# Soft mixture-of-experts stage: moving the softmax-maximum turns and the denominator products to other places of the TensorE order

## The reference, cut to what matters

```
x = layernorm(x) * norm_g + norm_b
se = (layernorm(slot_embeds) * slot_g + slot_b) * scale          # 16 experts x 64 slots
logits   = einsum('bnd,esd->bnes', x, se)
dispatch = softmax(logits, axis=1)                               # over the tokens
combine  = softmax(logits over all 1024 slots)                   # over experts and slots
slots = einsum('bnd,bnes->besd', x, dispatch)
gate  = gelu(slots @ Wg + bg);  up = slots @ Wu + bu             # 256 hidden features
eout  = (gate * up) @ Wd + bd
out   = einsum('bns,bso->bno', combine, eout);  x = x + tanh(g) * out
```

## Time and profile before

| | |
|---|---|
| timed runs | 1477.87, 1479.05, 1482.19 us; median 1479.05 |
| profiled execution, span of core 0 | 1498.2 us (no other time of that execution is at hand) |
| PE busy | 1377.6 us, 92% of the span |
| PEld busy | 1171.5 us, 78% |
| DVE busy | 953.4 us, 64% |
| ACT busy | 1012.3 us, 68% |
| POOL busy | 523.2 us, 35% |
| mean granted TensorE clock | 0.982 |

### The profile page before, as it was taken

How to read it: one execution, slowest core, us unless ns; L and a number is a source line. 1 busy time by engine, 2 the same in 40 slices (tenths; PEclk the granted TensorE clock), 3 DMA queues, 4 the chain that set the end, 5 groups by cost and what they waited for, 6 DMA issues and landing times. The chain is left out here.

```text
span 1498.2 us, 33716 instructions
## 1 busy us (share of the span) xinstructions
PE 1377.6 (92%) x12029; PEld 1171.5 (78%) x12029; DVE 953.4 (64%) x2374; ACT 1012.3 (68%) x2019; POOL 523.2 (35%) x510
## 2 busy tenths in 40 slices
PE   5898699899999999999999999988999999876985
PEld 4887588788888888888888888877778888755773
DVE  6998767666766767667667666552455555654455
ACT  5887487577677676776776767647788888633552
POOL 3112355322322322323223223302235555635553
PEclk9999899999999999999999999999999999998998
DMA  8300100399940000000000000022000000022236
GB/s 221 88 1 1 58 2 1 77 176 102 102 30 2 2 1 2 2 2 2 2 2 1 2 1 2 1 73 57 1 29 14 17 16 16 30 69 63 76 97 174
DMA packets 124980, 60.46 MB, mean 40 GB/s; under 512 B 41945, under 2 KB 120241, under 8 KB 124690
## 3 DMA queue, kind: packets, MB, share of 16 engines
q1 hardware_dynamic: 120274, 48.92, 18.2%
q0 software_dynamic: 4544, 9.38, 1.9%
HBM read 28.84 MB, written 29.44 MB: 39 GB/s over the span
## 5 line engine op out<-in xcount | busy, mean ns | idle before, releaser
L1349 DVE SCALAR_TENSOR_TENSOR hidden<-psU,b_cols,gelu 128x512 f32<-128x512 f32 x256 | 191.4, 750 | 170.1 <-ACT gelu L1474 104.9
L1474 ACT ACTIVATE gelu<-psG,b_cols 128x512 f32<-128x512 f32 x256 | 176.2, 689 | 109.6 <-PE psG L142 96.2
L1296 POOL TENSOR_TENSOR combine_sum<-combine_sum,combineT 128x512 f32<-128x512 f32 x48 | 63.3, 1319 | 294.9 <-ACT combineT L1488 294.9
L1325 POOL TENSOR_TENSOR dispatchT<-dispatchT,dispatch_inv 128x512 f32<-128x512 f32 x64 | 67.7, 1057 | 232.6 <-DVE dispatch_inv L1453 232.6
L1608 PE MATMUL psU<-w_down,hidden 128*64 128x128 f32 x2048 | 123.4, 273 | 0.0
L1608 PE MATMUL psDown<-w_down,hidden 128*64 128x128 f32 x2048 | 122.7, 273 | 0.0
L1861 POOL TENSOR_TENSOR probs<-probs,row_sum 128x512 f32<-128x512 f32 x64 | 66.2, 1035 | 143.6 <-DVE row_sum L1974 142.6
L1608 PEld LDWEIGHTS psU<-w_down,hidden 128*64 128x64 f32 x2048 | 113.2, 137 | 1.3 <-issue 1.2
L1608 PEld LDWEIGHTS psDown<-w_down,hidden 128*64 128x64 f32 x2048 | 113.9, 137 | 0.1
L140 PE MATMUL psG<-slots_hi,w_gate_hi 128*128 128x512 f32 x256 | 105.9, 414 | 1.1 <-ACT gelu L1474 0.6
L2038 ACT ACTIVATE probs<-psS,neg_max 128x128 f32<-128x128 f32 x256 | 91.2, 384 | 22.8 <-DVE neg_max L1971 18.4
(11 more groups left out here) (406 smaller groups left out, 3617.6 us busy)
## 6 DMA issues: line engine op xcount, KB each, us to landing
sorted_x<-empty_rows SPq DMA_DIRECT2D x1, 12736.0 KB, 77.5
tile_rows<-sorted_x SPq DMA_DIRECT2D x78, 65.0 KB
sorted_x<-empty_rows SPq DMA_DIRECT2D x1, 4544.0 KB, 29.9
expert_ys<-expert_y SPq DMA_DIRECT2D x16, 256.0 KB, 3.7
x<-in_x SPq DMA_DIRECT2D x8, 256.0 KB, 5.9
ctx<-in_ctx SPq DMA_DIRECT2D x8, 256.0 KB, 5.9
w_gate_raw<-in_L_ffn_Wg SPq DMA_DIRECT2D x1, 2048.0 KB, 10.9
w_up_raw<-in_L_ffn_Wu SPq DMA_DIRECT2D x1, 2048.0 KB, 16.1
```

Of the source, the lines that this page charges most:

```text
L1325: pool.tensor_tensor(e[:], e[:], over(rb[:], SEQ, 2), ALU.mult).then_inc(s["eb_normed"], 1)
L1349: dve.scalar_tensor_tensor(hid[e][:, half, :], U[half][:], bcol[:, 1, 4 * ch + 2 * e + half:][:, 0:1], gel[half][:], ALU.add, ALU.mult).th ...
L1474: act.activation(gel[half][:], G[half][:], ACT.Gelu, bias=bcol[:, 0, 4 * ch + 2 * e + half:][:, 0:1]).then_inc(s["gelu"], 1)
```

## The change

It moves work; no product, copy or reduction is added or removed. There are three moves.

- Scores: `AHEAD` goes from `(), (), (0,), (1, 2), (3,), (4, 5), (6,), (7,)` to `(), (), (0, 1), (2, 3), (4, 5), (6,), (7,), ()`, so that chunk 7 makes no score chunk, and the maximum over all eight is there when chunk 7 begins.
- Maxima: in chunk 7, `top` is turned right behind the turn of dispatch, into `M[:, 0]`; DVE's `mtok` stands between `expert_out` of the chunk before and the first `hidden`; the spread stands between `gate_up` of the second expert's halves, into `M[:, 1]`, and ACT's copy to `mb` between the last two gelu.
- Denominators: their products stand behind the last `gate_up` and ahead of the slots product, and go into `DN`; DVE's two instructions follow directly behind its last `hidden`; the first `down` of the chunk waits for the reciprocal.

In the head of octet -1, which has no experts' work, order and banks stay as they were.

```diff
-    AHEAD = ((), (), (0,), (1, 2), (3,), (4, 5), (6,), (7,))
+    AHEAD = ((), (), (0, 1), (2, 3), (4, 5), (6,), (7,), ())
...
+        def top_bank(o):
+            return M[:, 0, :] if has_core(o) else G[0][:]
+        def max_bank(o):
+            return M[:, 1, :] if has_core(o) else G[1][:]
...
 (vector engine, a chunk in order)
                     if has_core(o) and exists(o, ch, -1):
                         expert_out(k - 1, 1, (ch - 1) % CH)
+                    if ch == CH - 1 and has_head(o) and has_core(o):
+                        top_max(o)
...
                         hidden(k, 1, ch, 0)
                         hidden(k, 1, ch, 1)
+                    if has_core(o) and ch == CH - 1:
+                        need(dve, s["den"], o + 1)
+                        need(dve, s["x_new"], o)
+                        dve.reciprocal(ra[:], DN[:, 0, 0:OP]).then_inc(s["den_inv"], 1)
+                        need(dve, s["den_inv"], o + 1)
+                        dve.tensor_scalar(ra[:], ra[:], c.gates[:, 1:2], None, ALU.mult).then_inc(s["den_gated"], 1)
...
-                    if ch == CH - 1 and has_head(o):
-                        need(dve, s["top_t"], o + 2)
-                        need(dve, s["mb"], o + 1)
-                        dve.tensor_reduce(mtok[:], G0, AX.X, ALU.max).then_inc(s["mtok"], 1)
+                    if ch == CH - 1 and not has_core(o):
+                        top_max(o)
...
-                    if has_core(o) and ch == CH - 1:
-                        need(dve, s["den"], o + 1)
-                        need(dve, s["x_new"], o)
-                        dve.reciprocal(ra[:], U[0][:, 0:OP]).then_inc(s["den_inv"], 1)
...
 (scalar engine)
+            def max_rows(o):
+                need(act, s["mb"], o + 2)
+                need(act, s["ct_sub"], 8 * (o + 1))
+                act.copy(mb[:], max_bank(o)).then_inc(s["mb_ready"], 1)
...
+                        if ch == CH - 1 and has_head(o):
+                            max_rows(o)
                         gelu(k, 1, ch, 1)
...
 (tensor engine)
+            def top_turned(o):
+                need(pe, s["lb_max"], 8 * (o + 2))
+                for t in range(OP):
+                    last = pe.transpose(top_bank(o)[:, t * P:(t + 1) * P], top[:, t * P:(t + 1) * P], c.ident[:])
+                last.then_inc(s["top_t"], 1)
+            def top_spread(o):
+                need(pe, s["mtok"], o + 2)
+                for t in range(OP):
+                    last = pe.matmul(max_bank(o)[:, t * P:(t + 1) * P], mtok[:, t:t + 1].to_broadcast([P, P]), ident_r[:],
+                                     start=True, stop=True)
+                last.then_inc(s["mb"], 1)
+            def denominators(o, k):
+                need(pe, s["ct_summed"], 7 * (o + 1))
+                need(pe, s["eo_ready"], 2 * k - 1)
+                need(pe, s["d_ready"], min(k + 2, LAST + 1))
+                for t in range(OP):
+                    last = pe.matmul(DN[:, 0, t:t + 1], total[:, t, :], ones[:], start=True, stop=True)
+                last.then_inc(s["den"], 1)
...
                 if g == 0:
                     need(pe, s["eo_ready"], 2 * k - 1)
                     need(pe, s["d_ready"], min(k + 2, LAST + 1))
+                    if ch == CH - 1:
+                        need(pe, s["den_inv"], k // CH + 1)
...
                         dispatch_turned(o, ch)
+                    last_of_core = ch == CH - 1 and has_head(o) and has_core(o)
+                    if last_of_core:
+                        need(pe, s["sl_lo"], 2 * (k + 1))
+                        top_turned(o)
...
+                        if last_of_core:
+                            pe.wait_ge(s["ident_r"], 1)
+                            top_spread(o)
                         gate_up(k, 1, ch, 1)
+                    if ch == CH - 1 and has_core(o):
+                        denominators(o, k)
                     if exists(o, ch, 1):
                         need(pe, s["d_ready"], k + 2)
+                        if last_of_core:
+                            need(pe, s["mb_ready"], o + 2)
...
```

More of the change, by code:

```diff
@@ L1368, in column_max, with top_max @@
                                   negate=True).then_inc(s["lb_max"], 1)
+            def top_max(o):
+                need(dve, s["top_t"], o + 2)
+                need(dve, s["mb"], o + 1)
+                dve.tensor_reduce(mtok[:], top_bank(o).rearrange("p (t s) -> p t s", t=OP), AX.X, ALU.max
+                                  ).then_inc(s["mtok"], 1)
             def finish(o):
@@ L1579, in gate_up @@
                 cols = slice(half * P, (half + 1) * P)
-                first = isinstance(k, int) and ch == 0 and e == 0
-                if first:
-                    need(pe, s["mtok"] if half == 0 else s["mb_ready"], k // CH + 1)
+                if k == 0 and e == 0:
+                    pe.wait_ge(s["mtok"] if half == 0 else s["mb_ready"], 1)
                 if ch == 2 and e == 0 and half == 1 and k // CH < OCTETS - 1:
@@ L1587, in gate_up @@
                 product3(pe, G[half][:], [w[:, 2 * ch + e, cols] for w in wg], x).then_inc(s["gate"], 1)
-                if first and half == 0:
-                    need(pe, s["den_inv"], k // CH)
                 if e == 0 and half == 1:
@@ L1673, in body @@
                         last.then_inc(s["tx"], 1)
-                    if ch == CH - 1 and has_head(o):
-                        need(pe, s["lb_max"], 8 * (o + 2))
-                        need(pe, s["gelu"], 4 * k + 3)
-                        for t in range(OP):
-                            last = pe.transpose(G0[:, t, :], top[:, t * P:(t + 1) * P], c.ident[:])
-                        last.then_inc(s["top_t"], 1)
-                    if ch == CH - 1 and has_core(o):
-                        need(pe, s["ct_summed"], 7 * (o + 1))
-                        need(pe, s["hidden"], 4 * k + 3)
-                        for t in range(OP):
-                            last = pe.matmul(U[0][:, t:t + 1], total[:, t, :], ones[:], start=True, stop=True)
-                        last.then_inc(s["den"], 1)
+                    if ch == CH - 1 and not has_core(o):
+                        top_turned(o)
                     if has_core(o):
                         down(k, 1, ch)
-                    if ch == CH - 1 and has_head(o):
-                        need(pe, s["mtok"], o + 2)
-                        need(pe, s["gelu"], 4 * k + 4)
+                    if ch == CH - 1 and not has_core(o):
                         pe.wait_ge(s["ident_r"], 1)
-                        for t in range(OP):
-                            last = pe.matmul(G[1][:, t * P:(t + 1) * P], mtok[:, t:t + 1].to_broadcast([P, P]), ident_r[:],
-                                             start=True, stop=True)
-                        last.then_inc(s["mb"], 1)
+                        top_spread(o)
                     if has_core(o):
```

2 lines of the change are left out of this document (removed).

## The result

The changed kernel takes 1485.85 us (median of 4 runs, 1484.9 to 1486.23), the one before 1479.9 (4 runs, 1477.87 to 1482.19). The ratio is 1.0033, with a 95% interval from 1.0016 to 1.0049: slower by 5.95 us. The forecast of 1483.3 was added up from 1479.05, the median of three of those runs; the fourth moved the median before by 0.85 us. The profiled run of the changed kernel has a span of 1483.2 us.

What follows compares the result with a forecast made beforehand. TensorE was taken to bound the kernel. The groups' -3.7 us and the octet borders' +7.9 us gave +4.2 us on 1479.05, so 1483.3 us, with a range from 1476 to 1489.

Steps and rivals of the forecast that it cites:

- the sign that had the largest chance: Whole kernel: slower beyond the 0.3% line, chance 0.45, against 0.42 for within it and 0.13 for faster.
- What bounds the block: Whole block: TensorE, busy in all of octet 3, sets the time by its work plus its few waits.
- Scores ahead: Chunks 2 to 7: eight score chunks per octet before and after, at the same price wherever they stand; sum 0.
- The three groups: Chunk 7, TensorE: turned `top`, denominators and spread cost less among 128*128 products; 0.50 us gained in each of seven octets.
- its two readings: Chunk 7: gaps beside the groups stay with the `down` and `combine` neighbours, gain 0.52 us, or travel with the groups, gain 0.
- Octet 7: Last octet: only the denominators move, leaving the place between the two `down`; about 0.2 us gained.
- The new waits of chunk 7: Chunk 7: waits for the spread, ACT's copy, the slots product and the reciprocal are all hidden; cost 0.
- The border: Chunk 0, octets 2 to 6: POOL's lead over TensorE shrinks, delaying `x_hat` and `hidden`; 1.32 us each, 6.6 in all.
- Octet 1: Octet 1: constants behind POOL's late product delay `expert_out` by 1.32 us; the groups gain 0.50.
- The border does not come free: Denies the rival for chunk 0 that `x_hat` no longer waits for all three POOL instructions: 1474.1 us, chance 0.13.
- The partial loss: DVE's tail of chunk 7 a little faster than in a common chunk, or smaller gaps: 1479 to 1481.5 us, chance 0.12.
- The larger loss: Whole kernel at 1486 to 1494 us, or 1487 if the groups' gaps travel along; chance 0.17.

Runs made afterwards that it cites:

- ahead_alone: Kernel before with only the list of score chunks moved ahead, maxima and denominators left in place: 1481.22 us, ratio 1.0017.
- ahead_pad_later: Kernel before with the score list moved ahead and the padding writes held back until octet 3's work is done: 1479.57 us, ratio 1.0003.
- den_alone: Kernel before with only the denominators moved ahead of the slots product: 1481.0 us, ratio 1.001.
- max_alone: Kernel before with scores and maxima moved, denominators left where they were: 1481.47 us, ratio 1.0023.
- xhat_later_before: Kernel before with DVE's four `x_hat` put behind the first two `hidden` of chunk 0: 1477.89 us, ratio 0.9996.
- all_pad_later: Changed kernel with POOL's two shifts early, octet 1's constants dealt out over its chunks, and padding writes held back: 1466.18 us, ratio 0.9905.
- xhat_later: Changed kernel with DVE's four `x_hat` put behind the first two `hidden` of chunk 0: 1474.44 us, ratio 0.9973.
- shifts_early: Changed kernel with POOL's two shifts of the next octet made at the end of chunk 7: 1474.18 us, ratio 0.9964.

## Why the prediction was right, and where it was off

The forecast of 1483.3 lies 2.6 us from the measured 1485.85, inside its range, with the sign that had the largest chance. Of the 2.6 us, 0.85 is the median of the kernel before (1479.9 for 1479.05); the forecast difference of +4.2 stands against +5.95 in the timed runs and +7.1 in the block's trace. Against the trace it lacks 2.9 us, with octet 1 alone 3.15 short; that the timed difference lies nearer is no merit of the working. Step by step:

- **What bounds the block.** Right: TensorE sets it. Each edit that closed a gap of TensorE showed its whole worth in the length of the octet.
- **Scores ahead, 0.** Right in octets 2 to 6 (102.34 before and in ahead_alone). Wrong in octet 1, by 1.5 us: a chunk's price was taken from octet 6, where the DMA share is 0.01, and carried to an octet with a share of 1.11, in which the padding is written and TensorE has a gap that ahead_pad_later does not have. Octet 0 costs 0.2 more.
- **The three groups, -0.50 each octet.** Right in size: chunk 7 takes 13.37 (forecast 13.4), a gain of 13.94 - 13.37 = 0.57. Of its two readings, that the gaps stay with the 128*64 neighbours held: den_alone and max_alone show gains that rise with the number of changes of shape taken away, and none for one of two neighbouring groups. Put down to the changes of shape, the gain is 0.14 us for each on average, an estimate from 0.57 for four.
- **Octet 7, -0.2.** Right: the end, from the last turn to the start of the last product, takes 23.57 instead of 23.81.
- **The new waits of chunk 7, 0.** Right: the 1.22 us in which TensorE stands in octet 3 are those of chunk 0's `hidden` (1.21 in the timeline of octet 2), and nothing is left for chunk 7.
- **The border, +1.32 in each of octets 2 to 6.** Right to the hundredth: POOL's product starts at T+0.73, the up product at T+5.31 (forecast 5.35), chunk 0 grows by 1.30. The end of `x_hat` follows the start of POOL's product by 398.82 - 394.95 = 3.87, as in the earlier trace rows. The runs showed in addition what that rests on: with two of the three POOL instructions taken away `x_hat` needs 1.49, and with `x_hat` behind `hidden` the price is nil.
- **Octet 1, +1.32 - 0.50.** This is the term that was mis-sized: it measured +3.97, 3.15 more. The wait grew as said, from 4.66 to 5.96. Behind it TensorE ran 6.8 instead of 3.3 us at the lower clock, with 0.63 more of busy time, for which the sum had no term. The longer wait is not shown as its cause: xhat_later_before and ahead_pad_later have 0.82 of full behind the old wait of 4.7 us. The remaining 2.6 us are in chunks 5 and 6, for which no term stood. ahead_alone, with only the scores moved, has 1.5 of them, ahead_pad_later and all_pad_later, with the padding's writes elsewhere, have none.
- **The sum.** -3.7 + 7.9 = +4.2 was forecast. The block has -0.57 x 7 - 0.24 = -4.2 for the groups, +1.31 x 6 = +7.9 for the border, +0.2 in octet 0, and 0.6 + 2.6 in octet 1: +7.1 within rounding.

**The rivals.** The border does not come free: `x_hat` went one by one between POOL's instructions again. Its price, 1474.1, is what xhat_later (1474.44) and shifts_early (1474.18) take, where that condition is brought about by another order. The partial loss did not occur. The larger loss, 1486 to 1494, did not come, and no run shows what its upper part would need: the longer stretch at the lower clock in octet 1 cost 0.63 us, and the 1.2 us waits at the borders left the clock at 1.00 in the windows of octets 2 and 3. That the gaps travel along is excluded by 13.37.

## What to carry to other kernels

Work that one takes off the bounding engine at the end of a stage can take away the head start of the others too, as here POOL's went from 0.59 us ahead of the turn to 0.73 behind: list what the next stage's first instructions wait for, and measure their lead against the bounding engine before and after. If a lead turns negative, look first at the order within the engine that is now late: here moving four small instructions behind the two that TensorE waits for turned a loss of 0.33% into a gain of 0.27%. The price of a chunk that was read in a quiet stretch need not hold elsewhere: the stage with the DMA traffic and the constants would have needed rows of its own.

## What the runs showed of the hardware

**`x_hat` and POOL's instructions went one by one.** In chunk 0 of octet 2 of the changed kernel the four `x_hat` take 0.72, 1.33, 1.32 and 0.33 us beside POOL's 1.04 and two of about 1.29; with POOL's three out of the way, in xhat_later, each takes 0.34. In these rows DVE gets exactly one `x_hat` done for each of POOL's three instructions. The second and the third begin 0.05 us behind the start of one of POOL's 1.29 us and end 0.08 us behind its end, with 1.33 and 1.32 us instead of 0.34. All four stand in a row in DVE's list, and POOL's next instruction still starts 0.05 us ahead of the next `x_hat`. A DVE instruction with two inputs in SBUF is held up as well in these traces: the shift of dispatch takes 0.68 us in chunks 1 to 7 of octet 2 of all_pad_later, and 1.70 in its chunk 0, where it starts 0.15 behind POOL's `x_normed` (timeline):

```profile
387.52 1.29 POOL L1352 TENSOR_TENSOR x_normed<-x_normed,norm_b 128x512 f32<-128x512 f32 x1
387.66 1.70 DVE L1455 TENSOR_TENSOR dispatchT<-logits,neg_max_d 128x512 f32<-128x512 f32 x1
```

Where the shift starts first, by 0.17, it takes 0.69, and POOL's `x_normed` takes 1.66 instead of 1.29 (xhat_later, octet 2):

```profile
397.99 0.69 DVE L1429 TENSOR_TENSOR dispatchT<-logits,neg_max_d 128x512 f32<-128x512 f32 x1
...
398.16 1.66 POOL L1323 TENSOR_TENSOR x_normed<-x_hat,norm_g 128x512 f32<-128x512 f32 x1 [1.14 <-DVE x_hat L1420]
```

**Gaps of TensorE without a releaser.** While 12.7 MB are written to `sorted_x`, octet 1 of seven of these kernels has nine gaps of 0.3 to 1.5 us that end 1.2 to 1.6 us after the end of a 16 KB packet of the instruction queue q8. With the writes held back to 605 to 739 us (ahead_pad_later) the 1.18 us gap of ahead_alone is gone, and none stands there. The working had no term for the writes. What they do to TensorE, and why only in octet 1, is not shown.

**The stretch at the lower clock.** In octet 1 the wait of 4.7 us has beside it a granted clock of 0.91 of full over chunk 0 (before, ahead_alone) or of 0.82 (xhat_later_before, ahead_pad_later), with 0.50 as the lower level in all four; TensorE's busy time is 13.54 in the first two and 14.65 and 14.31 us in the others. So the wait's length alone does not give the price of the slow stretch; in these rows that price differs by 0.8 to 1.1 us for one and the same wait.

**The groups among 128*64 weights.** With both groups and the four changes between 128*64 and 128*128 weights gone, chunk 7 takes 13.37 us instead of 14.66 - 0.72 = 13.94. That is 0.57, or 0.14 for each change: an estimate, as no run varied the shape alone. Taking out one of two groups that stand side by side between such changes gained nothing (den_alone, 14.66 before and after).
